# Four graph layers on a 4096-node adjacency: projections of passes 3, 4, 5 and 8 moved by one unit of matrix work

## What is computed

```python
def _gwnn_layer(features, wavelets, wavelets_inv, W, filt):     # layer 0, run twice, relu between
    xw = features @ W
    spec = wavelets_inv @ xw
    spec = filt[:, None] * spec
    return wavelets @ spec
# layer 1
h = jnp.concatenate([input, adj @ input], axis=1) @ weight
# layer 2
messages = node_features @ W_msg + b_msg
logits = (messages @ W_q) @ (messages @ W_k).T / scale + gate_bias
gates_masked = sigmoid(logits) * adj_matrix * recency_prior      # both are adj: adj squared
updated = relu(concatenate([node_features, gates_masked @ messages], axis=1) @ W_upd + b_upd)
# then a layer norm with gamma and beta
# layer 3
x1 = swish((adj @ x) @ W + b)
x2 = swish((adj @ x1) @ W + b)
# around each layer
x = _layernorm(x + layer(x, adj, ...), axis=-1)
```

## Time and profile before

| | before |
|---|---|
| median of three runs | 1665.4 us (1662.06 to 1670.98) |
| the profiled execution, its own time | 1666.21 us |
| its span | 1664.4 us |
| PE busy | 1609.0 us, 97% of the span |
| DVE busy | 1212.8 us, 73% |
| ACT busy | 1099.7 us, 66% |
| POOL busy | 54.2 us, 3% |
| HBM read and written | 414.09 MB and 69.21 MB |

### The profile page before, as it was taken

The page is one execution under the profiler, slowest core; times in us unless marked ns, Lnnn a source line. Parts: engine busy times, 40 slices in busy tenths (PEclk is TensorE's granted clock), DMA queues, the critical chain, the costliest instruction groups (busy, mean ns, idle before and its releaser), DMA issues. The chain is left out here.

```text
span 1664.4 us, 19276 instructions
## 1 busy us (share of the span) xinstructions
PE 1609.0 (97%) x7674; PEld 767.7 (46%) x7674; DVE 1212.8 (73%) x1181; ACT 1099.7 (66%) x784; POOL 54.2 (3%) x49
## 2 busy tenths in 40 slices
PE   7999999999999998999999899999999999999997
PEld 4444444444444444444554444444353444444443
DVE  6866538654766478556899598998989986554886
ACT  5667747764878567755667487796878786454743
POOL 2000000000000000000000000100000100000001
PEclk9999999999999999999999999999999999999999
DMA  9979798979799888996878354554545898764972
GB/s 368 414 301 381 284 419 345 371 284 415 286 388 426 340 317 346 382 340 270 321 283 315 129 202 177 177 207 172 201 166 190 322 371 304 268 250 162 363 276 109
DMA packets 67562, 484.56 MB, mean 291 GB/s; under 512 B 7712, under 2 KB 7872, under 8 KB 9232
## 3 DMA queue, kind: packets, MB, share of 16 engines
q1 hardware_dynamic: 66240, 478.70, 74.6%
q0 software_dynamic: 1088, 4.56, 0.8%
q10 hardware_dynamic: 144, 0.07, 0.0%
HBM read 414.09 MB, written 69.21 MB: 290 GB/s over the span
## 5 line engine op out<-in xcount | busy, mean ns | idle before, releaser
L989 DVE SCALAR_TENSOR_TENSOR a_lo<-a_ring,a_hi 128x2048 f16<-128x2048 f32 x320 | 723.9, 2288 | 301.1 <-ACT a_hi L792 296.9
L792 ACT ACTIVATE a_hi<-a_ring 128x2048 f16<-128x2048 f32 x320 | 604.9, 1905 | 279.4 <-PE spare L594 153.2
L594 PE MATMUL acc<-a_hi,y_hi 128*128 128x512 f16 x1536 | 460.5, 381 | 5.5 <-ACT a_hi L792 3.5
L594 PE MATMUL acc<-a_hi,y_lo 128*128 128x512 f16 x1536 | 460.4, 381 | 0.0
L606 PE MATMUL acc<-a_lo,y_hi 128*128 128x512 f16 x1536 | 406.0, 379 | 7.9 <-DVE a_lo L998 4.9
L606 PEld LDWEIGHTS acc<-a_lo,y_hi 128*128 128x128 f16 x1536 | 149.7, 98 | 192.6 <-DVE a_lo L998 8.1
L594 PEld LDWEIGHTS acc<-a_hi,y_lo 128*128 128x128 f16 x1536 | 150.8, 98 | 182.8 <-issue 2.9
L594 PEld LDWEIGHTS acc<-a_hi,y_hi 128*128 128x128 f16 x1536 | 150.5, 98 | 183.2 <-issue 8.1
L1011 DVE SCALAR_TENSOR_TENSOR gates<-gates,a_ring 128x1024 f32<-128x1024 f32 x128 | 156.1, 1220 | 35.1 <-ACT gates L822 34.8
L805 ACT ACTIVATE a_hi<-gates 128x1024 f16<-128x1024 f32 x128 | 134.8, 1053 | 41.1 <-DVE gates L1011 40.9
L998 DVE TENSOR_TENSOR a_lo<-gates,a_hi 128x1024 f16<-128x1024 f32 x128 | 155.8, 1217 | 0.0
(11 more groups left out here) (119 smaller groups left out, 763.6 us busy)
## 6 DMA issues: line engine op xcount, KB each, us to landing
a_ring<-adj_dram SPq DMA_DIRECT2D x326, 1024.0 KB, 7.4
saved_squares<-squares SPq DMA_DIRECT2D x64, 1024.0 KB, 12.7
a_ring<-saved_squares SPq DMA_DIRECT2D x64, 1024.0 KB, 4.8
x_T<-xt_dram SPq DMA_DIRECT2D x4, 512.0 KB, 8.1
x_rows<-x_dram POOLq DMA_DIRECT2D x1, 2048.0 KB, 12.8
out_dram<-x_rows POOLq DMA_DIRECT2D x3, 512.0 KB, 3.0
out_dram<-x_rows SPq DMA_DIRECT2D x2, 256.0 KB, 2.0
w<-W_dram POOLq DMA_DIRECT2D x2, 64.0 KB, 5.2
```

Of the source, the lines that this page charges most:

```text
L594: mm = pe.matmul(sums[:, h * BANK:(h + 1) * BANK], blk(y[:, y_pass % 2, :], st.j0 + s), slot(a_hi, st)[:, s, h * BANK:(h + 1) * BANK], sta ...
L792: act.activation(slot(a_hi, st), loaded(st), ACT.Copy, scale=2.0 ** A_EXP).then_inc(s_ahi, 1)
L989: dve.scalar_tensor_tensor(out=slot(a_lo, st).rearrange("p s c -> p (s c)"), in0=loaded(st).rearrange("p s c -> p (s c)"), scalar=2.0 ** A ...
```

## The change

The projection of a finished chunk is issued one unit later in passes 3, 4, 5 and 8. Everything of the same epilogue behind it moves with it on PE, ACT, DVE and POOL, and `LENGTH` of these passes grows by one. `z_T` stays at stage 0. Because an epilogue is longer, the next chunk's may start later: (4,1) starts at unit 232 and not 231, (5,1) at 295 and not 294, (5,2) at 306 and not 304, (8,1) at 554 and not 553, (8,2) at 564 and not 562. `KEPT` names other steps: two of pass 8's kept steps come at units 553 and 554, not 552 and 553, and two at 563 and 564, not 561 and 562; the last two stay. SP's order and the number of steps stay as they are.

```diff
-KEPT = [... for i, j, t in ((0, 0, 1), (0, 0, 2), (0, 2, 2), (0, 2, 3), (1, 3, 0), (1, 3, 1))]
+KEPT = [... for i, j, t in ((0, 0, 3), (0, 3, 0), (0, 2, 2), (0, 2, 3), (1, 3, 1), (1, 3, 2))]
...
-LENGTH = {0: 1, 1: 4, 2: 3, 3: 3, 4: 7, 5: 10, 6: 23, 7: 4, 8: 9, LAST_GATED: 14}
+LENGTH = {0: 1, 1: 4, 2: 3, 3: 4, 4: 8, 5: 11, 6: 23, 7: 4, 8: 10, LAST_GATED: 14}
...
# PE
-                4: {1: [project], 7: [x_transposes]},
+                4: {2: [project], 8: [x_transposes]},
...
# DVE
-                4: {0: [take_over], 1: [values, ln_moments(0, s_val, "val"), normalise], 5: [y_low]},
+                4: {0: [take_over], 2: [values, ln_moments(0, s_val, "val"), normalise], 6: [y_low]},
```

More of the change, by code:

```diff
@@ L118 @@
 Unit = namedtuple("Unit", "step p k use s first last")
-KEPT = [(i, (j * GROUP + t) * SJ) for i, j, t in ((0, 0, 1), (0, 0, 2), (0, 2, 2), (0, 2, 3), (1, 3, 0), (1, 3, 1))]
+KEPT = [(i, (j * GROUP + t) * SJ) for i, j, t in ((0, 0, 3), (0, 3, 0), (0, 2, 2), (0, 2, 3), (1, 3, 1), (1, 3, 2))]
 def plan():
@@ L570, in _ @@
                 2: {2: [project]},
-                3: {1: [project]},
-                4: {1: [project], 7: [x_transposes]},
-                5: {1: [project], 5: [x_transposes], 6: [messages], 7: [queries], 9: [message_rows]},
+                3: {2: [project]},
+                4: {2: [project], 8: [x_transposes]},
+                5: {2: [project], 6: [x_transposes], 7: [messages], 8: [queries], 10: [message_rows]},
                 6: {3: [project]},
                 7: {1: [project]},
-                8: {2: [project]},
+                8: {3: [project]},
                 LAST_GATED: {1: [project]},
@@ L772, in _ @@
                 2: {0: [evacuate, relu_z], 2: [y_high]},
[L773 to L776, removed]
+                3: {0: [evacuate], 3: [y_high]},
+                4: {0: [evacuate], 6: [y_high], 8: [save_x_T]},
+                5: {0: [evacuate], 6: [save_x_T], 7: [save_m_T], 8: [qk_high(0, kT_hi, K_EXP)],
+                    9: [qk_high(1, qT_hi, Q_EXP)], 10: [y_high]},
                 6: {1: [evacuate], 5: [relu], 20: [normalise_again(range(HB))], 21: [normalise_again(range(HB, CB))],
@@ L779, in _ @@
                 7: {0: [evacuate], 2: [silu], 3: [y_high]},
-                8: {0: [evacuate], 2: [silu]},
+                8: {0: [evacuate], 3: [silu]},
                 LAST_GATED: {0: [evacuate], 3: [relu], 11: [normalise_again(range(CB))], 14: [y_high]},
@@ L972, in _ @@
                 2: {0: [take_over], 2: [y_low, split_biases]},
-                3: {0: [take_over], 1: [values], 2: [y_low]},
-                4: {0: [take_over], 1: [values, ln_moments(0, s_val, "val"), normalise], 5: [y_low]},
-                5: {0: [take_over], 1: [values], 2: [ln_moments(0, s_val, "val"), normalise],
-                    7: [qk_low(0, kT_hi, kT_lo, K_EXP)], 8: [qk_low(1, qT_hi, qT_lo, Q_EXP)], 9: [y_low, add_beta]},
+                3: {0: [take_over], 2: [values], 3: [y_low]},
+                4: {0: [take_over], 2: [values, ln_moments(0, s_val, "val"), normalise], 6: [y_low]},
+                5: {0: [take_over], 2: [values], 3: [ln_moments(0, s_val, "val"), normalise],
+                    8: [qk_low(0, kT_hi, kT_lo, K_EXP)], 9: [qk_low(1, qT_hi, qT_lo, Q_EXP)], 10: [y_low, add_beta]},
                 6: {8: [ln_moments(0, s_nl, "nonlin")], 10: [times_gamma], 13: [affine_residual],
@@ L979, in _ @@
                 7: {3: [y_low]},
-                8: {0: [take_over], 4: [residual], 5: [ln_moments(0, s_res, "resid")], 6: [normalise]},
+                8: {0: [take_over], 5: [residual], 6: [ln_moments(0, s_res, "resid")], 7: [normalise]},
                 LAST_GATED: {4: [ln_moments(0, s_nl, "nonlin")], 5: [times_gamma], 6: [affine_residual],
@@ L1064, in store @@
                 pool.dma_start(out[:, i * CB:(i + 1) * CB, :], x_chunk(p, k)).then_inc(s_out, 16)
-            stages = {4: {1: [root(0)]}, 5: {2: [root(0)]}, 6: {8: [root(0)], 16: [root(1)]}, 8: {5: [root(0)], 6: [store]},
+            stages = {4: {2: [root(0)]}, 5: {3: [root(0)]}, 6: {8: [root(0)], 16: [root(1)]}, 8: {6: [root(0)], 7: [store]},
                       LAST_GATED: {4: [root(0)], 8: [root(1)]}}
```

## The result

The changed kernel takes 1654.19 us (median of five executions, 1652.39 to 1654.81), the kernel before 1664.98 us (five, 1662.06 to 1670.98): a ratio of 0.9925, with a 95% interval from 0.9912 to 0.9939. In a later series it was 1654.61 us and 0.9929 (0.9914 to 0.9943). The forecast was 1656.5 us, between 1650.5 and 1664.5. The profiled execution took 1654.23 us with a span of 1652.4 us, 12.0 us less than before.

What follows compares the result with a forecast made beforehand. PE, busy 97% of the span, bounds the kernel; only its 55 us of idle time or low-clock matmuls can give time. Terms summed to 9.2 us off the profiled 1666.2 us; forecast 1656.5 us, range 1650.5 to 1664.5.

Steps and rivals of the forecast that it cites:

- (3,0): Pass 3, first chunk: PE's stall for `z_T` ahead of the projection goes, 1.7 us gained.
- (4,0) and (4,1): Pass 4, first two chunks: shorter waits for a low half and `z_T`, no low clock; 4.5 us gained.
- (4,3): Pass 4, last chunk: `y_lo` moves with the norm block and comes late for unit 280, 0.9 us lost.
- (8,1) and (8,2): Pass 8: both stalls for `z_T` ahead of the projections go, 3.6 us gained.
- (4,2): Pass 4: norm block lacks cover; a new low-half wait loses 1.7 us, a low clock behind it another 1.7.
- (5,0): Pass 5, first chunk: the `z_T` stall and the slow project behind it go, 4.1 us gained.
- rival (a): The loads bind: gains of passes 4 and 5 come back as waits for `a_hi`, 1666.8 us; chance 0.21.
- (5,0) to (5,2), and the second logits: Pass 5: stall ahead of (5,1) goes, 1.2 us gained; late gates make the second logits wait, 1.6 us lost.
- (5,3) and pass 6: Stalls at gates and a norm block stay: 0, up to 1.7 us either way from the clock.
- (b): More than the sum: (4,2) escapes its wait or low clock, pass 6 loses one; 1651 to 1654 us; chance 0.12.
- (c): Norm blocks moved in passes 4 and 5 find no cover, 3.4 us each at eight: 1679 us; chance 0.06.
- (d): `z_T` comes later by as much as PE, so stalls keep their length: 1666 us; chance 0.04.

Runs made afterwards that it cites:

- Pass 3 alone: Only pass 3's stages and `LENGTH` as changed, all else as in the kernel before: 1663.92 us, ratio 0.9986.
- pass 4 alone: Only pass 4's stages and `LENGTH` as changed, all else as in the kernel before: 1663.72 us, ratio 0.9981.
- pass 8 alone: Only pass 8's stages, its `LENGTH` and the new `KEPT`, all else as in the kernel before: 1661.83 us, ratio 0.9972.
- the early block: The changed kernel, but (4,2) and (4,3) keep the stages and length of before: 1649.62 us, ratio 0.9900 to the kernel before.

## Why the prediction came out

**Where the time comes from.** The forecast's sum was 9.2 us, the profiled stretches give 13.9, and 1.9 were lost at the start. Waits make up most of it, low clocks the rest: those at (4,1) and (5,0), and one in pass 6. That the time came so near is in part luck. Two places where the clock did not fall, in (4,2) and in pass 6, gave 3.4 us that the sum did not have, and the start took 1.9 of them back. The other terms give 10.5 us for 9.2.

**(3,0), (4,0) and (4,1), (4,3), (8,1) and (8,2)** came out within 0.2 us. Pass 3 alone and pass 4 alone show that the first three need nothing of the rest; pass 8 alone gives 3.35 for the 3.6.

**(4,2).** The new wait is 2.06 us where 2.2 was expected, and the early block shows its cause. The other half of the term failed: I charged 1.7 us for a low clock, on stalls of 2.12 and 2.26 us. In the changed kernel's two profiles there was none, with pass 4 alone there was.

**(5,0)** gave 4.35 for 4.1. What ends that stall is a load, which the step did not say. So rival (a) has a true core: the loads set `z_T` there, and with (4,1) two units later they are what leaves DVE idle. But a unit of cover was enough, and no gain came back as a wait for `a_hi`.

**(5,0) to (5,2), and the second logits.** The wait at the logits, 1.46 + 0.17 us, is the 1.6 predicted. The 1.2 us ahead of it were too low: the first profile's stretch around (5,1) gives 1.9. I had charged 0.3 to 0.5 us each at the message rows and x_transposes; the wait at the message rows is 0.32 us, as before, and x_transposes have none.

**(5,3) and pass 6, "0":** 1.7 us more came from the clock behind the 2.12 us stall. That it could was allowed for, the direction was not.

**The kept steps.** "The two kept steps lie behind the moved norm block again and cover it" was wrong: nothing there needed cover. The term of 3.6 us holds without them.

**The rivals.** (b) stood for more than the sum by the clock. Two of its three terms of 1.7 us happened, no low clock at (4,2) and one less in pass 6; with 1.9 us lost at the start the time came to its upper edge, 1654, where it meets the forecast's range. (c) did not: only (4,2) lacked its cover. But it is real: with (4,1) two units later DVE idles ahead of the block, and most of the gain at (4,1) is lost. With all of pass 4 two units later the loss is another, `y_lo` behind one more low half. The 15.7 us that (c) calls gained are 15.1 by the terms of the sum (1.7 + 4.5 + 4.1 + 1.2 + 3.6), which changes nothing in what it says. (d) holds nowhere in the change.

## What to carry to other kernels

Moving a step behind a unit of matrix work buys that unit's time only where PE waits there; it costs one low half, and the wait for its inputs, at every chunk it is applied to. So choose the distance for each place, and look at what the engine that must run the moved block will do first, and whether that item's own input will be loaded and split by then. A wait named after one engine may be ended by a load two engines up: follow the chain before pricing what removes it. Where a stall may or may not be followed by a low clock, keep that 1.7 us as a term of its own in the range, and compare terms by stretch of the trace rather than by medians that the clock moves.

## What the hardware showed that I had not expected

Stalls of the same length were followed by a low clock or not. There are 14 profiles: those of the twelve runs, of the kernel before and of the changed kernel. Every stall from 2.55 to 4.20 us in passes 4 and 5 had one (11 of 11); that of 2.12 us in pass 6 in 8 of 14, that of 2.25 in 8 of 14; that of 2.06 us in (4,2) in 1 of 5; that of 2.00 us in pass 7 in none of 14. None of 1.7 us or less had one, but one of 1.91 us did. Each cost 1.7 us where a pair with and without it can be compared (in pass 6, 22.80 us against 21.10 from one stall to the next). What decides it is open. The kernel before ranged from 1660.17 to 1672.45 us over the 53 executions beside these runs, the changed one from 1652.39 to 1655.02 over 11; that fewer long stalls leave less to chance is my reading and not tested, and the load ahead of (5,0) has its share in that spread.
